# Issuing every fourth spread of dt*x one step early, as a pair, in a fused two-layer decoder on one core

## What is computed

```python
x = layernorm(x + L0_attn(x))        # selective state-space scan, 1024 channels, 16 states each
x = layernorm(x + L0_xattn(x, side, ctx))   # int8-style quantised expert, 4 of them
x = layernorm(x + L0_ffn(x))         # gated feed-forward, hidden 2048
x = layernorm(x + L1_attn(x))        # token-mixing recurrence, 32 heads
x = layernorm(x + L1_xattn(ctx, x))  # selective scan, 512 channels, 16 states each
x = layernorm(x + L1_ffn(x))         # 8 routed experts of 352 (top 2) and a shared one of 1408
```

```python
h[d, n, t] = exp(dt[d, t] * A[d, n]) * h[d, n, t-1] + dt[d, t] * x[d, t] * B[n, t]
y[d, t] = sum_n h[d, n, t] * C[n, t]
```

## Time and profile before

| | us |
|---|---|
| median of 3 runs | 3944.65 (3939.63 to 3953.14) |
| the profiled execution, its own time | 3938.74 |
| its span (first to last instruction) | 3937.0 |
| PE busy | 3515.4 (89%) |
| DVE busy | 3180.0 (81%) |
| ACT busy | 1623.4 (41%) |
| POOL busy | 1347.1 (34%) |
| the three expert stages with a scan, from the span's start | 1010 to 1350, 1895 to 2235, 2780 to 3120 |

### The profile page before, as it was taken

How to read it: one execution, slowest core, us unless ns; L and a number is a source line. 1 busy time by engine, 2 the same in 40 slices (tenths; PEclk the granted TensorE clock), 3 DMA queues, 4 the chain that set the end, 5 groups by cost and what they waited for, 6 DMA issues and landing times. The chain is left out here.

```text
span 3937.0 us, 41370 instructions
## 1 busy us (share of the span) xinstructions
PE 3515.4 (89%) x15406; PEld 1471.1 (37%) x15406; DVE 3180.0 (81%) x2733; ACT 1623.4 (41%) x2201; POOL 1347.1 (34%) x493
## 2 busy tenths in 40 slices
PE   5777779989999979999999989998999989977998
PEld 1222243334333443334333443334433443324444
DVE  5999569888999869788999869888999869795333
ACT  5666343224655353224655343224655353213001
POOL 3455304362344304352344304352344304351000
PEclk9888899999899999989999999999899999988999
DMA  6678402221233302221233302221233302110322
GB/s 231 244 278 299 174 17 73 76 72 57 87 100 104 132 27 73 76 65 64 88 104 101 132 27 73 76 69 61 87 100 105 132 27 73 57 41 17 104 97 73
DMA packets 105430, 382.94 MB, mean 97 GB/s; under 512 B 14224, under 2 KB 27920, under 8 KB 102800
## 3 DMA queue, kind: packets, MB, share of 16 engines
q1 hardware_dynamic: 83632, 342.57, 25.5%
q10 hardware_dynamic: 21600, 37.73, 3.4%
HBM read 290.80 MB, written 64.32 MB: 90 GB/s over the span
## 5 line engine op out<-in xcount | busy, mean ns | idle before, releaser
L300 PE MATMUL ps<-r,ring 128*128 128x512 bf16 (+1 forms) x2040 | 780.8, 383 | 0.0
L297 PE MATMUL ps<-xr,ring 128*128 128x512 bf16 x1568 | 613.8, 391 | 0.3 <-PEq L1853 0.3
L301 PE MATMUL ps<-xr,ring 128*128 128x512 bf16 x1568 | 610.8, 390 | 0.0
L297 PE MATMUL ps<-r,ring 128*128 128x512 bf16 (+2 forms) x1384 | 546.8, 396 | 50.2 <-DVE xc L1107 17.9
L301 PE MATMUL ps<-r,ring 128*128 128x512 bf16 (+2 forms) x1384 | 545.5, 395 | 0.0
L1159 POOL TENSOR_TENSOR hh<-hh,bc 128x2048 f32<-128x2048 f32 x72 | 334.8, 4650 | 512.3 <-DVE hh L1069 512.3
L1159 POOL TENSOR_TENSOR bc<-bc 128x2048 f32<-128x2048 f32 x64 | 304.3, 4755 | 344.5 <-DVE bc L1069 344.5
L1159 POOL TENSOR_TENSOR r<-r,bc 128x2048 f32<-128x2048 f32 x56 | 261.3, 4667 | 298.5 <-DVE r L1069 298.5
L1069 DVE TENSOR_TENSOR_SCAN hh<-da,hh 128x2048 f32<-128x2048 f32 x72 | 325.6, 4523 | 1.2
L1110 DVE TENSOR_TENSOR xc<-xc,ps 128x512 f32<-128x512 f32 x176 | 119.5, 679 | 226.7 <-PE ps L301 226.7
L1069 DVE TENSOR_TENSOR_SCAN bc<-da,bc 128x2048 f32<-128x2048 f32 x64 | 296.3, 4630 | 0.5
(11 more groups left out here) (271 smaller groups left out, 6552.5 us busy)
## 6 DMA issues: line engine op xcount, KB each, us to landing
ring<-wsplit SPq DMA_DIRECT2D x216, 768.0 KB, 4.3
r<-wstream SPq DMA_DIRECT2D x54, 768.0 KB, 7.5
ring<-wsplit SPq DMA_DIRECT2D x76, 512.0 KB, 4.0
wsplit<-ring SPq DMA_DIRECT2D x38, 768.0 KB, 4.8
da<-r ACTq DMA_DIRECT2D x360, 63.9 KB, 2.1
wsplit<-r SPq DMA_DIRECT2D x14, 768.0 KB, 5.0
r<-wstream SPq DMA_DIRECT2D x19, 512.0 KB, 6.3
r<-xT SPq DMA_DIRECT2D x7, 1024.0 KB, 4.8
```

What stands on the lines that cost most here:

```text
L297: mm = pe.matmul(out, w_hi, x_hi, start=start, stop=False)
L300: pe.matmul(out, w_hi, x_lo, start=False, stop=False)
L301: return pe.matmul(out, w_lo, x_hi, start=False, stop=stop)
```

## The change

In the expert stage the spread of block s = 4, 8, ..., 28 (function `early_spread`) is issued in step s-2 instead of step s-1, right behind the spread of block s-1, and goes into `y_bank` instead of `dtx_bank`. `inputs(s)` of VectorE reads it there. The waits follow: the early spread waits for `finish_y` of two quads before (`yout`) instead of for `inp`; the spread after it waits for one block less; `reduce_quad` waits in addition until `inputs(4j+4)` has read `y_bank`. Since the early spread needs the next tile's dt*x one step sooner, `inputs_of` moves from the end of steps 2, 6, ... to the end of steps 1, 5, .... The stages "first" and "ffn" keep their order.

```diff
--- before.py
+++ after.py
@@ -830,6 +830,13 @@
         HELD = 2 * CHUNK
         dt_bank, dtx_bank, y_bank = [k.ps[:, i, :] for i in range(3)]
 
+        def early_spread(s):
+
+            return gated and s % 4 == 0 and 4 <= s < blocks
+
+        def input_bank(s):
+            return y_bank if early_spread(s) else dtx_bank
+
         def last_chunk(p):
             return p >= pieces - KM
 
@@ -882,8 +889,11 @@
 
             def spread_dtx(s):
 
-                if s >= 1:
-                    pe.wait_ge(inp, s)
+                if early_spread(s):
+                    if s >= 8:
+                        pe.wait_ge(yout, s // 4 - 1)
+                elif s >= 1:
+                    pe.wait_ge(inp, s - 1 if early_spread(s - 1) else s)
                 at = slice(32 * (s % 4), 32 * (s % 4) + 32)
                 if which == 0:
                     if s // 4 + 1 > made:
@@ -891,11 +901,13 @@
                     source = k.dtx_now[at, s // 4 % 2, :]
                 else:
                     source = dtx[at, s // 4, :]
-                pe.matmul(dtx_bank, k.headmean[at, :], source, start=True, stop=True).then_inc(dtx_mm, 1)
+                pe.matmul(input_bank(s), k.headmean[at, :], source, start=True, stop=True).then_inc(dtx_mm, 1)
 
             def reduce_quad(j):
 
                 pe.wait_ge(read, 4 * j + 4)
+                if early_spread(4 * j + 4):
+                    pe.wait_ge(inp, 4 * j + 5)
                 if j >= 1:
                     pe.wait_ge(yout, j)
                 for n in range(GRP):
@@ -967,8 +979,10 @@
                 spread_weights(0)
 
             for step in range(steps):
-                if 2 <= step + 1 < blocks:
+                if 2 <= step + 1 < blocks and not early_spread(step + 1):
                     spread_dtx(step + 1)
+                if early_spread(step + 2):
+                    spread_dtx(step + 2)
                 if step + 2 < blocks and not carried:
                     spread_dt(step + 2)
                 if gated and 1 <= step < tiles:
@@ -1056,7 +1070,7 @@
                 dve.wait_ge(dtx_mm, s + 1)
                 if s >= NB:
                     dve.wait_ge(reduced, (s - NB) // 4 + 1)
-                dve.tensor_tensor(quartet(s), dtx_bank[:, None, :].broadcast_to([P, GRP, T]), k.in_rows, ALU.mult).then_inc(inp, 1)
+                dve.tensor_tensor(quartet(s), input_bank(s)[:, None, :].broadcast_to([P, GRP, T]), k.in_rows, ALU.mult).then_inc(inp, 1)
 
             def inputs_of(j):
 
@@ -1139,7 +1153,7 @@
                 if carried and step == 1:
                     half = slice(J // 2, J)
                     dve.tensor_tensor(dt[:, half, :], dt[:, half, :], dtx[:, half, :], ALU.add).then_inc(late_sum, 1)
-                if which == 0 and step % 4 == 2 and step + 2 < blocks:
+                if which == 0 and step % 4 == (1 if gated else 2) and step // 4 * 4 + 4 < blocks:
                     inputs_of(step // 4 + 1)
 
         @blk.gpsimd
```

## The result

The change makes the kernel faster. The medians are 3925.22 us with it and 3947.41 us before (8 runs each, taken side by side); the ratio is 0.9958 with a 95% interval of 0.9943 to 0.9973, so 16.6 us less (10.7 to 22.5). Two further series of the same kernel, taken on other occasions, gave 0.9965 (0.9951 to 0.9978) and 0.9963 (0.9948 to 0.9977). The forecast was 13.8 us less.

What follows compares the result with a forecast made beforehand. TensorE was taken to bound the expert stages, VectorE close behind; 1.05 us per quad, capped by VectorE's take, gave 4.8 + 4.3 + 4.7 = 13.8 us, so 3944.65 - 13.8 = 3930.8 us, range 3922 to 3945.

Steps and rivals of the forecast that it cites:

- TensorE bounds the stage, VectorE is close behind: Expert stage, 1053 to 1340 us: TensorE busy 287.00 of 287.00 us, VectorE 274.66; savings come off VectorE's 28.7 us of stalls.
- A second spread is free beside the first: New pair of spreads: the second adds 0.01 us, as in an ffn stage, so 1.05 us per quad is saved.
- rival 2: The two spreads, each with two waits, run serially: gain 0, median stays at 3944.65 us; chance 0.16.
- Rival 3: Second spread starts with the first's second record: 0.52 us saved per quad, 8.6 us in all, median 3936; chance 0.07.
- the room of its quad: How far TensorE can come forward before the down piece of step 4j+3 meets VectorE's take; 0.49 us in step 7.
- What the missing spread saves, 1.05 us: Head of steps 3, 7, ... 27: the spread's 1.05 us of TensorE's queue goes, 7 times a stage.
- the upper bound: Saving that also counts some 0.1 us for the tile-shape change around the removed spread; not booked in the sum.
- The take of step 4j+3 holds part of it back: Down pieces wait for VectorE's take, which caps the saving at 4.8, 4.3 and 4.7 us in the three stages.
- TensorE's new waits for the take, 5 us in all: Before the down pieces of steps 7, 11, ... 27: new short TensorE waits, 18.9 - 13.8 = 5 us together.
- Step 2 and the clock: Early spread waits for `inputs_of(1)`, some 4 us of TensorE; old waits paid earlier, no VectorE stall before step 9.
- rival 4: TensorE goes cold after step 2's idle time, staying at the low clock some 20 us: slower, median 3957; chance 0.06.
- `inputs_of` costs VectorE the same at either place: Moving its 0.68 us from the end of step 4j+2 to 4j+1 is free: once per quad, between the same stalls.

Runs made afterwards that it cites:

- Experiment 2: The change, with the early spread issued behind the gate's 12 matmuls so that it has no partner: ratio 1.0000 to the kernel before, first expert stage 314.5 us.
- experiment 5: The change plus VectorE's take of the down piece ahead of `inputs`: ratio 0.9960 to the kernel before, stages of 309.4, 307.8 and 306.2 us.
- experiment 6: The kernel before, with only VectorE's take of the down piece moved ahead of `inputs`: ratio 0.9997, stages of 314.2, 313.5 and 313.8 us.
- experiment 9: The change with `inputs_of` at the end of steps 0, 4, ..., VectorE's take left in place: ratio 0.9965 to the kernel before, stages of 308.8 us.
- experiment 1: The kernel before with only `inputs_of` moved one step earlier, every spread in its old place: ratio 0.9986, stage 314.4 us.
- experiment 4: The change without its first early spread (block 4), `inputs_of(1)` left in step 2: ratio 0.9980 to the kernel before, stages of 309.9, 310.0 and 309.9 us.

## Why the prediction was right

- **TensorE bounds the stage, VectorE is close behind.** Right. The saving came out of VectorE's stalls, one for one: 13.9 us of stalls, 14.0 us of the three stages (4.8, 4.4 and 4.7, where 4.8, 4.3 and 4.7 were booked).
- **A second spread is free beside the first.** Right: 1.06 us for four records, in 17 of 18 pairs as far as their records are kept. Experiment 2 shows that this, and not the earlier place, is the gain, and that rival 2 is out: the form with two waits behaves like the one with one wait. Rival 3, in-order starts of single records, would have given 8.6 us. The rule itself, which the Trainium skill states for matmuls ("TensorE: Matmul & The Clock Gate", Part 3), is contradicted less than the prediction says: taken for whole spreads it holds in these pairs, whose second spread starts 0.01 us after the first. It is the two records of one f32 spread that don't stay together. The one pair that took 1.57 us lost nothing at the end, since the room of its quad was 0.49 us.
- **What the missing spread saves, 1.05 us.** A little small. The product that came 1.37 us ahead of the routing weights with the spread between them is now 0.22 ahead: 1.15 us, the upper bound. It mattered little: only two quads had more room than 1.05 us. The stall of step 17 fell from 2.00 to 0.88 us, its room being 1.09. That of step 21, with a room of 1.41, fell by 1.05 us, since in step 19 the routing weights are a matmul of 32 columns: this one, too, starts 0.31 us after the last product and not 0.22 (1204.26 and 1204.57 with the change), so the 0.1 us of the tile shape stays.
- **The take of step 4j+3 holds part of it back.** Right, and the term that decided the size. The stalls of steps 9, 13, 17, 21, 25 and 29 of the first stage fell by 0.46, 0.95, 1.12, 1.05, 0.76 and 0.55 us where 0.49, 0.95, 1.05, 1.05, 0.74 and 0.54 were booked. Experiments 5, 6 and 9 show the limit from the other side. One term is right for a reason that was not seen: the saving booked for step 7 (0.49, 0 and 0.33 us) comes as well from the early `inputs_of(1)` without any pair (experiment 1). The pairs by themselves are worth the 4.4 us a stage between experiment 1 and the change, 13.2 us of the 14.0. As both causes meet the same limit, the sum came out all the same.
- **TensorE's new waits for the take, 5 us in all.** Too small. The profile puts 4.0, 3.6 and 3.6 us of TensorE's idle time down to VectorE's takes, 11.2 us in all. Most of it lies in steps 3 to 7 (3.2, 2.7 and 2.7 us). The prediction took the wait of step 2 as the old one paid earlier, but the old waits of steps 2 and 3 were 4.97 and 1.53 us and the new one is 4.12. So TensorE comes 2.4 us ahead and stands in front of the next down pieces instead. It costs nothing, since VectorE has no stall there.
- **Step 2 and the clock.** Right that it is free: experiment 4. The wait of 4.12 us is where it was said to be, and VectorE stalls nowhere before step 9. The fall of the clock that rival 4 feared does come, but it is short: in windows of 2 us of the first stage the granted clock is 0.50 from 1034 to 1040 and 0.95 from 1040 to 1042, 6 us where it stood at 0.50 for 10 us before.
- **`inputs_of` costs VectorE the same at either place.** Right for steps 4j+1 and 4j+2, but it stops short: experiment 9 shows that at step 4j it is cheaper, as it fills the stall. For TensorE the early place is no pure move: `inputs_of(1)` a step sooner brings 0.8 us in the three stages by itself (experiment 1).
- **The rest of the 16.6 us.** Between the profiles, 14.0 of the 15.5 us are in the three stages. The other 1.5 us are a sum of shifts of up to 5 us in both directions in code that did not change. So the 14.0 us confirm the 13.8 of the sum, while the 16.6 us of the ratio, the 22.2 us between the medians and the median of 3925.2 us against the 3930.8 of the forecast hold a part that the prediction does not explain; that they come out near it is in part luck.

## What to carry to other kernels

If two engines are nearly equally full, a saving on the one that bounds is worth, at each handover, no more than the slack that the other leaves there. So list the handovers between two stalls and read the room at each: this gave every quad here to 0.1 us (once by a cause that was not seen). And once a saving is held back, look for work of the other engine that can move from behind its stall to ahead of it: that brought another 4.0 us a stage here, by two edits that on the kernel before are worth 0.9 and 0.3 us a stage.

## What was not expected

The code between the last scan of an expert stage and the first scan of the next ffn stage, which no kernel here touches, takes from 156.5 to 164.0 us, and with it goes TensorE's granted clock. Busy time by window over that stretch, of the kernel before and of experiment 4 (columns as in the earlier trace rows):

```profile
1328.70:1485.20 156.50, 129.48 (x624) 65.69 (x623) 111.08 (x162) 67.18 (x104) 20.32 (x14) 0.95 0.19 68
2213.50:2375.60 162.10, 134.82 (x625) 68.30 (x624) 111.08 (x163) 67.24 (x104) 20.45 (x14) 0.91 0.18 66
3100.40:3259.80 159.40, 133.17 (x624) 67.82 (x623) 111.88 (x163) 67.18 (x104) 20.15 (x14) 0.92 0.19 67
```

```profile
1321.60:1483.40 161.80, 136.17 (x615) 70.40 (x623) 112.30 (x163) 67.24 (x104) 20.14 (x14) 0.88 0.18 66
2209.40:2373.20 163.80, 135.11 (x615) 69.64 (x623) 112.11 (x162) 67.25 (x104) 20.15 (x14) 0.90 0.18 65
3096.70:3258.30 161.60, 135.99 (x615) 70.24 (x622) 112.15 (x161) 67.25 (x104) 20.15 (x14) 0.88 0.18 66
```

In the profile of experiment 4 these three stretches take 9.2 us more than before (487.2 against 478.0), against 14.2 us that its three stages gained. That execution was one of the slower of its eleven (3939.9 us, the median is 3933.7). Over whole executions it is the same: in a series of 23 runs of the kernel before, the time goes with the mean granted clock with a correlation of -0.96, from 3931.8 us at 0.943 to 3960.2 us at 0.932. The matmuls in the later part of these stretches stand in short groups with waits between them. In windows of about 10 us of the first stretch before TensorE is busy for 2.9 to 10 us and the granted clock lies between 1.00 and 0.50, so some groups run at the upper of its two levels and some at the lower one. At comparable places (120 us from its start) the clock is 1.00 before and 0.60 in experiment 4. Why some kernels meet the low level more often (experiment 4 has a median clock of 0.937, experiment 1 one of 0.942) was not tried and stays open. By the intervals above, it limits what a ratio of this kernel can tell to about 0.2%, and is why the stage lengths were used.
